# Last layer's edges: one scan per half in place of 14 steps, and one float32 product in place of three bf16 ones

## The reference

```python
msgs = z[edge_dst] @ Wd + z[edge_src] @ Ws + edge_weight[:, None] * ww[None, :] + bm
agg = jax.ops.segment_max(msgs, edge_dst, num_segments=n)
```

## Time and profile before

| | |
|---|---|
| median of three runs | 5489.27 us (5487.87 to 5501.67) |
| the profiled execution | 5497.03 us |
| its span, first to last instruction | 5495.1 us |
| granted TensorE clock, mean over the span | 0.679 |
| the stage of the change | from 4320.9 us to 5420.9 us |

### The profile page before, as it was taken

How to read it: one execution, slowest core, us unless ns; L and a number is a source line. 1 busy time by engine, 2 the same in 40 slices (tenths; PEclk the granted TensorE clock), 3 DMA queues, 4 the chain that set the end, 5 groups by cost and what they waited for, 6 DMA issues and landing times. The chain is left out here.

```text
span 5495.1 us, 57053 instructions
## 1 busy us (share of the span) xinstructions
PE 1987.8 (36%) x9749; PEld 986.7 (18%) x9749; DVE 3681.4 (67%) x8459; ACT 1834.0 (33%) x5828; POOL 3746.1 (68%) x2991
## 2 busy tenths in 40 slices
PE   2699999997600000000020000000002445566555
PEld 1354444443300000000010000000001212222222
DVE  9676666664578878878875666666666545555555
ACT  0333333332338878877820000000001312222221
POOL 0688888887177777777536888888883365556563
PEclk9899999999855555555555555555555777777777
DMA  9555555555337666665635555555552223222222
GB/s 403 154 105 98 102 92 101 101 92 107 95 101 261 226 239 220 241 246 217 233 130 166 169 169 175 176 169 169 170 174 89 64 85 95 91 90 92 90 92 72
DMA packets 283515, 819.47 MB, mean 149 GB/s; under 512 B 63270, under 2 KB 178486, under 8 KB 271251
## 3 DMA queue, kind: packets, MB, share of 16 engines
q1 hardware_dynamic: 99250, 504.98, 25.0%
q0 software_dynamic: 171504, 252.10, 21.1%
q10 hardware_dynamic: 12528, 60.37, 2.7%
HBM read 368.73 MB, written 448.51 MB: 149 GB/s over the span
## 5 line engine op out<-in xcount | busy, mean ns | idle before, releaser
L1864 POOL DMA_INDIRECT arena<-table,arena x784 | 989.9, 1263 | 238.8 <-issue 238.8
L624 POOL DMA_INDIRECT tab<-arena x560 | 988.5, 1765 | 188.8 <-issue 142.7
L746 PE MATMUL psum<-arena 128*128 128x512 bf16 (+1 forms) x4704 | 957.9, 359 | 0.0
L2348 POOL DMA_INDIRECT arena<-table,arena x676 | 651.3, 963 | 425.7 <-issue 201.8
L1514 PE MATMUL psum<-ident,arena 128*128 128x128 f32 x15 | 3.7, 425 | 2525.1 <-DVEq L1542 2525.1
L1287 POOL DMA_INDIRECT arena<-table,arena x588 | 713.1, 1213 | 189.5 <-issue 177.4
L2411 PE MATMUL psum<-arena 128*128 128x512 bf16 x2025 | 588.5, 443 | 378.4 <-issue 272.6
L1333 ACT ACTIVATE arena<-arena 128x128 f32<-128x128 f32 x1974 | 598.5, 388 | 187.4 <-DVE arena L1441 141.9
L1441 DVE SCALAR_TENSOR_TENSOR arena<-arena 128x512 f32<-128x512 f32 x728 | 545.1, 749 | 13.8 <-issue 1.5
L746 PEld LDWEIGHTS psum<-arena 128*128 128x128 bf16 x4704 | 435.8, 99 | 479.8 <-issue 35.6
L1514 PEld LDWEIGHTS psum<-ident,arena 128*128 128x128 f32 x15 | 2.7, 212 | 2525.7 <-DVEq L1542 2525.5
(11 more groups left out here) (406 smaller groups left out, 4207.0 us busy)
## 6 DMA issues: line engine op xcount, KB each, us to landing
rows<-arena SPq DMA_DIRECT2D x56, 3808.0 KB
arena<-seg_rows SPq DMA_DIRECT2D x112, 896.0 KB
rows<-arena SPq DMA_DIRECT2D x56, 1008.0 KB
seg_rows<-arena ACTq DMA_DIRECT2D x28, 1792.0 KB
rows<-arena SPq DMA_DIRECT2D x56, 896.0 KB
arena<-table,arena POOLq DMA_INDIRECT x2048
arena<-src_lanes SPq DMA_DIRECT2D x56, 448.0 KB
tab<-arena POOLq DMA_INDIRECT x560
```

Source lines behind the costliest of these rows:

```text
L624: eng.indirect_dma_start(out=m.tabs[j], out_offset=bass.IndirectOffsetOnAxis(ap=idx[g][:, k:k + 1], axis=0), in_=rows[g][:, k, 0:D], in_of ...
L746: t = eng.matmul(ps[:, c, 0:w], part[n // 2 % PAIRS][:, n % 2, :], hot[n % HOTS][:, lo:lo + w], start=False, stop=False, skip_group_check= ...
L1864: eng.indirect_dma_start(out=kv[k][:, j, :], out_offset=None, in_=m.table2, in_offset=bass.IndirectOffsetOnAxis(ap=idx[k][:, j:j + 1], axi ...
L2348: eng.indirect_dma_start(out=feat[h][:, j, :], out_offset=None, in_=m.table3, in_offset=bass.IndirectOffsetOnAxis(ap=idx[h][:, j:j + 1], a ...
```

## The change

The messages of a half lie feature by feature, with 15 places each: place 0 carries the last maximum of the other half, places 1 to 14 are the edges. One `tensor_tensor_scan` over all 128 x 15 places of a partition (add the reset, take the maximum with the message) gives all states of the half; a reset of -1e30 at place 0 separates the features. ScalarE spreads the resets over the features (`spread_resets`) and writes the states back edge by edge for the store (`turn_back`). The one-hots become float32, and each block's product is one float32 matmul with the table itself; `split` and its three tiles go. ScalarE's order in a turn becomes: scalings of half 0, states of the last half, resets, eviction, indices of half 0, scalings of half 1, states of half 0, resets, indices of half 1 (`next_indices` is `stage` renamed). In VectorE's `half` one one-hot stands ahead of the scan and the others behind it.

```diff
--- before.py
+++ after.py
...
-        msg = A(HALF, D)
+        msg = A(D, HALF + 1)
+        maxima = [A(D, HALF + 1) for _ in range(2)]
         rows = [A(HALF, D) for _ in range(2)]
         tab = A(NB, D)
-        parts = [A(NB, D, dt=BF16) for _ in range(3)]
         keys = A(BATCH, dt=F16)
-        hot = [A(BATCH, dt=BF16) for _ in range(NB)]
+        hot = [A(BATCH) for _ in range(NB)]
         turned_rows = A(BATCH)
-        resets, vals, act_vals = A(BODY), A(BODY), A(BODY)
+        resets = [A(D, HALF + 1) for _ in range(2)]
+        act_vals = A(BODY)
...
                 def store(i, h):
-                    hold(eng, scanned, i * BODY + (h + 1) * HALF + 1)
+                    hold(eng, turned_back[h], i + 1)
                     eng.dma_start(lanes(m.rows3)[:, bass.ds(i * BODY + h * HALF, HALF), :], rows[h]).then_inc(stored[h], 16)
 
+                for h in range(2):
+                    eng.nop().then_inc(stored[h], 16)
...
-                def split():
-                    for k, (a, b) in enumerate(TAB_HALF):
-                        eng.wait_ge(tab_in[k], 16)
-                        eng.activation(parts[0][:, a:b, :], tab[:, a:b, :], ACT.Copy).then_inc(high_made, 1)
-                    for k, (a, b) in enumerate(TAB_HALF):
-                        eng.wait_ge(rest_made, k + 1)
-                        eng.activation(parts[1][:, a:b, :], tab[:, a:b, :], ACT.Copy).then_inc(mid_made, 1)
-
-                def stage(i, h, before):
+                def next_indices(i, h, before):
...
+                        if not isinstance(i, int):
+                            eng.wait_ge(found_summed, i * FOUND - FOUND + 1)
...
+                def spread_resets(i, h):
+
+                    hold(eng, scanned, 2 * i + h)
+                    eng.activation(resets[h][:, :, 1:HALF + 1],
+                                   spread(m.reset[:, bass.ds(i * BODY + h * HALF, HALF)], 1, [P, D, HALF]), ACT.Copy).then_inc(spread_out[h], 1)
+
+                def turn_back(i, h):
+
+                    eng.wait_ge(scanned, 2 * i + h + 2)
+                    eng.wait_ge(stored[h], 16 * i + 16)
+                    eng.activation(rows[h], maxima[h][:, :, 1:HALF + 1].rearrange("p f t -> p t f"), ACT.Copy).then_inc(turned_back[h], 1)
+
+                eng.wait_ge(begun, 2)
+                spread_resets(0, 0)
+                spread_resets(0, 1)
                 scale(0, 0, HALF)
-                split()
-                stage(0, 0, HALF)
+                next_indices(0, 0, HALF)
                 scale(0, 1, HALF)
-                stage(0, 1, HALF)
+                turn_back(0, 0)
+                spread_resets(1, 0)
+                next_indices(0, 1, HALF)
                 with eng.Fori(1, TURNS) as i:
                     scale(i, 0, HALF)
-                    stage(i, 0, i * HALF + HALF)
-                    scale(i, 1, HALF - FOUND)
+                    turn_back(i - 1, 1)
+                    spread_resets(i, 1)
                     eng.wait_ge(hot_used, i * NB + NB)
                     eng.wait_ge(turned, i)
                     eng.activation(turned_rows, found, ACT.Copy).then_inc(evicted, 1)
-                    stage(i, 1, i * (HALF - FOUND) + HALF)
+                    next_indices(i, 0, i * HALF + HALF)
+                    scale(i, 1, HALF - FOUND)
+                    turn_back(i, 0)
+                    spread_resets(i + 1, 0)
+                    next_indices(i, 1, i * (HALF - FOUND) + HALF)
+                turn_back(TURNS - 1, 1)
...
-                eng.wait_ge(low_made, 2)
+                for k in range(2):
+                    eng.wait_ge(tab_in[k], 16)
...
-                        for p, part in enumerate(parts):
-                            t = eng.matmul(found, part[:, b, :], hot[b], start=(b == 0 and p == 0), stop=(b == NB - 1 and p == 2))
-                        t.then_inc(hot_used, 1)
...
                 f = Steps(eng, begun)
-                f.then(eng.memset(rows[1][:, HALF - 1, :], -BIG))
-                eng.engine_nop().then_inc(weighed, 1)
+                for h in range(2):
+                    f.put(eng.memset(resets[h], -BIG))
+                f.then(eng.memset(maxima[1], -BIG))
+                eng.engine_nop().then_inc(found_summed, 1)
...
-                def split():
-
-                    for k, (a, b) in enumerate(TAB_HALF):
-                        eng.wait_ge(high_made, k + 1)
-                        eng.tensor_tensor(tab[:, a:b, :], tab[:, a:b, :], parts[0][:, a:b, :], ALU.subtract).then_inc(rest_made, 1)
-                    for k, (a, b) in enumerate(TAB_HALF):
-                        eng.wait_ge(mid_made, k + 1)
-                        eng.tensor_tensor(parts[2][:, a:b, :], tab[:, a:b, :], parts[1][:, a:b, :], ALU.subtract).then_inc(low_made, 1)
...
-                def stage(i):
-                    eng.wait_ge(scanned, i * BODY + 1)
-                    eng.nop(nofuse=True)
-                    eng.tensor_copy(resets, m.reset[:, bass.ds(i * BODY, BODY)]).then_inc(marked, 1)
-                    eng.tensor_copy(vals, m.val[:, bass.ds(i * BODY, BODY)]).then_inc(marked, 1)
-                    eng.wait_ge(marked, 2 * i + 2)
-
                 def half(i, h, n, before, hots):
 
+                    eng.wait_ge(scanned, 2 * i + h + 1)
+                    eng.tensor_copy(msg[:, :, 0], maxima[1 - h][:, :, HALF]).then_inc(carried, 1)
                     eng.wait_ge(landed[h], 16 * before)
                     eng.wait_ge(scaled, 2 * i + h + 1)
-                    eng.wait_ge(scanned, i * BODY + h * HALF + 1)
-                    eng.tensor_tensor(msg[:, 0:n, :], feat[h][:, 0:n, :], scaled_w[:, 0:n, :], ALU.add).then_inc(summed, 1)
+                    by_edge = msg.rearrange("p f t -> p t f")
+                    eng.tensor_tensor(by_edge[:, 1:n + 1, :], feat[h][:, 0:n, :], scaled_w[:, 0:n, :], ALU.add).then_inc(summed, 1)
                     if n < HALF:
                         eng.wait_ge(turned, i + 1)
-                    for j in range(n, HALF):
-                        s = h * HALF + j
-                        eng.scalar_tensor_tensor(out=msg[:, j, :], in0=m.edge_w[:, :], scalar=vals[:, s:s + 1],
-                                                 in1=rows_found[:, j - n, :], op0=ALU.mult, op1=ALU.add).then_inc(weighed, 1)
+                        eng.wait_ge(vals_staged, i + 1)
+                        for j in range(n, HALF):
+                            s = h * HALF + j
+                            eng.scalar_tensor_tensor(out=by_edge[:, j + 1, :], in0=m.edge_w[:, :], scalar=act_vals[:, s:s + 1],
+                                                     in1=rows_found[:, j - n, :], op0=ALU.mult, op1=ALU.add).then_inc(found_summed, 1)
+                    for hot_of in hots[:1]:
+                        one_hot(*hot_of)
+                    eng.wait_ge(spread_out[h], i + 1)
+                    eng.wait_ge(carried, 2 * i + h + 1)
                     eng.wait_ge(summed, 2 * i + h + 2)
-                    for j in range(HALF):
...
-                        eng.wait_ge(scanned, i * BODY + s + 1)
-                        if j == 0 and not (isinstance(i, int) and i == 0):
-                            eng.wait_ge(stored[h], 16 * i)
-                        if j == n:
-                            eng.wait_ge(weighed, i * FOUND + 1)
-                        eng.scalar_tensor_tensor(out=rows[h][:, j, :], in0=rows[h][:, j - 1, :] if j else rows[1 - h][:, HALF - 1, :],
-                                                 scalar=resets[:, s:s + 1], in1=msg[:, j, :], op0=ALU.add, op1=ALU.max).then_inc(scanned, 1)
-                        if j < len(hots):
-                            one_hot(*hots[j])
+                    if n < HALF:
+                        eng.wait_ge(found_summed, i * FOUND + 1)
+                    eng.wait_ge(turned_back[h], i)
+                    eng.tensor_tensor_scan(maxima[h].rearrange("p f t -> p (f t)"), resets[h].rearrange("p f t -> p (f t)"),
+                                           msg.rearrange("p f t -> p (f t)"), -BIG, ALU.add, ALU.max).then_inc(scanned, 1)
+                    for hot_of in hots[1:]:
+                        one_hot(*hot_of)
 
...
-                stage(0)
...
-                split()
...
-                eng.wait_ge(scanned, TURNS * BODY + 1)
-                f.then(eng.tensor_copy(m.lane_end[:, 0:D], rows[1][:, HALF - 1, :]))
+                eng.wait_ge(scanned, 2 * TURNS + 1)
+                f.then(eng.tensor_copy(m.lane_end[:, 0:D], maxima[1][:, :, HALF]))
```

More of the change, by code:

```diff
@@ L2301, in layer3_edges @@
         tab_in = [sem(f"table_landed{k}") for k in range(2)]
[L2302 removed]
         keys_in, hot_made, hot_used = sem("keys_landed"), sem("one_hots_made"), sem("one_hots_used")
         evicted, turned = sem("rows_evicted"), sem("rows_turned")
[L2305 removed]
         vals_staged, scaled = sem("weights_staged"), sem("weights_scaled")
[L2307 removed]
+        spread_out = [sem(f"resets_spread{h}") for h in range(2)]
```

(8 more changed lines are left out.)

8 lines of the change are left out of this document (1 added, 7 removed).

## The result

| | kernel before | kernel changed |
|---|---|---|
| median of 4 runs | 5488.57 us (5484.47 to 5501.67) | 5534.23 us (5529.28 to 5546.23) |
| profiled execution | 5497.03 us, span 5495.1 | 5546.23 us, span 5544.5 |
| stage, first gather to last | 4321.9 to 5397.1: 1075.2 us | 4331.0 to 5456.3: 1125.3 us |
| turn, mean of 26 | 39.17 us | 1048.30 / 26 = 40.32 us |

The ratio is 1.0082, 95% interval 1.0059 to 1.0106: slower by 0.8%. The 50.1 us between the first gather and the last are the whole difference of the spans, 49.4 us.

What follows compares the result with a forecast made beforehand. It took GpSimd's gathers plus 8.3 us of waits per turn as the stage's bound. A turn of 30.9 + 3.7 = 34.6 us saves 119 us, the ends 8: 5489 - 127 = 5362, rounded 5360 us; range 5265 to 5580.

Steps and rivals of the forecast that it cites:

- GpSimd's own turn: GpSimd's time per turn without its waits, 24 gathers of 1.25 us included: 30.9 us, before and after the change.
- E: Rival, slower: gathers wait while float32 one-hots are written, 6.5 us per turn; +42 us, 5530 us; chance 0.03.
- fall of 4.6 us per turn: The stage's turn goes from 39.17 to 34.6 us; 26 turns give 119 us less.
- tail: GpSimd's wait per turn for late signals, eviction, staging and first gather: 3.7 us in place of 8.3.
- The late signals: VectorE's signalling operations per turn fall from 61 to 33; priced per signalling instruction, its idle time falls by 26/61.
- A: Rival, faster: GpSimd never waits and the 8.3 us per turn go altogether; -224 us, 5265 us; chance 0.17.
- Scan 4.3 us: VectorE: each of two scans per turn over 128x1920 takes 4.3 us, 8.6 us for both.
- One-hot 0.47: VectorE: a one-hot of 512 elements written in float32 takes 0.47 us; 25 add 2.0 us per turn.
- D: Rival, slower: float32 one-hots take 0.68 us on VectorE, turn 44 us; +117 us, 5605 us; chance 0.07.
- C: Rival, slower: TensorE becomes the bound, turn 45.3 us at 1.2 GHz throughout; +151 us, 5640 us; chance 0.21.
- B: Rival: the stall belongs to gathers in flight, not VectorE's instruction count; only the ends gain, 5480 us; chance 0.14.
- The ends: Start and end of the stage: -7.5 us by dropping the three-way split, nothing from the last turn; 8 us less.

Runs made afterwards that it cites:

- Scans alone: Changed kernel with the bf16 one-hots, three-way split and three bf16 products of before: 5449.0 us (kernel before beside it 5249.2) and 5444.5 us (5500.7).
- messages in PSUM: Changed kernel with the scan reading its messages from PSUM and its resets from SBUF, float32 one-hots and products kept: 5302.0 us (ratio 1.0097), again 5331.1 us (1.0026).
- PSUM and bf16: Changed kernel with the scan's messages in PSUM, bf16 one-hots and three bf16 products per block: 5254.0 us (ratio 0.9997), 5242.3 us (0.9972), 5517.2 us (1.0030).
- unstruck: Kernel before, unchanged, in the faster of its two conditions: 5253.7 us profiled, 30.30 us per turn; struck means the condition where it takes about 5490 us.
- The scan in 8 pieces: Changed kernel with each scan made as eight over 16 features: 5443.1 us (ratio 0.9912); with bf16 one-hots and three bf16 products, 5294.3 us (1.0072).

## Why the prediction failed

**Its direction was wrong; its range, 5265 to 5580 us, held the 5534.** The step that failed is GpSimd's own turn, which the sum, the forecast and every rival but E carried over as 30.9 us (24 gathers x 1.25 = 30.0, and 0.9 more). It became 24 x 1.675 = 40.2 us. Scans alone and the messages in PSUM show that the scan's second SBUF input makes 7.3 us of it and the float32 one-hots 2 to 3. The forecast's fall of 4.6 us per turn became a rise of 1.15.

**Why I missed it.** I costed the scan by VectorE's time alone, and looked for a claim on GpSimd only in the one-hots. The steps that the scan replaces had two SBUF inputs too, but at 0.35 us each they held a gather for little in that trace (three of 676 took over 3 us); one instruction of 4.15 us holds it for all of that. I then gave rival E 0.03 since gathers took 963 ns beside today's one-hots: a row of bf16 one-hots can't show what float32 ones do. E's 5530 us was right to 4 us by luck: it had 6.5 us per turn of one-hots and a tail of 3.7 us, where there are 2.7 of one-hots, 7.6 of scans and no tail.

**The late signals.** I read 8.3 us of waits per turn as the kernel's and forecast 3.7 us to stay. In the changed kernel 4.3 / 26 = 0.2 us stayed, but my reason, fewer of VectorE's signals, is refuted by PSUM and bf16, which loses as much with 35 of them as the kernel before with 61. A's claim, a turn at GpSimd's floor and 5265 us, is what PSUM and bf16 and the kernel before show unstruck, not the changed one. The change took away one loss of 8.9 us per turn and put another of some 10 in its place, which is the measured +1.15 us per turn, 29.9 of the 50 us. The other 20 lie behind the window: the last gather ends 14.6 us after it in the changed kernel and ended 5.2 us ahead of its end in the kernel before. Against an unstruck kernel before, 5534 to 5249 would be 5% slower; that pair was never run side by side.

**The terms that held.** Scan 4.3 us, measured 4.15. One-hot 0.47, measured 0.487, which ends D, and is near the estimate from the Trainium skill (VectorE: DVE Perf Modes, The perf-mode tier table), 0.43. TensorE's share was 730.75 / 26 = 28.1 us per turn at a granted 0.80, so C did not come. B neither, in its form: GpSimd's waits went. (75 x 0.21 to 0.42 is 15.8 to 31.5 us, not 16.0 to 32.0; no term used it.)

**The terms that were off and cost nothing here.** The sum into the layout by features took 3.23 and 2.34 us, not 2.02 and 1.49; I had not priced its output's stride. The copies that turn the maxima back took 3.31 us, not 1.7 (the spreads did, 1.69). ScalarE's turn was 18.0 us, not 15.5. VectorE and ScalarE have 15 and 22 us of idle time in the turn, so neither counts. The ends were to give 8 us: behind the last gather it was 98.0 us and is 88.2, and the start of the stage moved by 9.1 between the two traces, which the stages ahead of it explain as well (it lies between 4309.6 and 4332.6 over all runs).

**A version that beats both.** None does in both conditions. Messages in PSUM with bf16 products is level with the kernel before in one unstruck set and 0.3% faster in the other, 0.3% slower where it is struck. Scans alone is 1.0% faster struck and 3.8% slower unstruck. The scan in 8 pieces is 0.9% faster struck, and with bf16 0.7% slower unstruck; neither was run in the other condition.

**What stays open.** What makes single instructions of VectorE, TensorE and SyncE late. All kernels whose time the condition raises have gathers near 0.95 us; those whose gathers are held have fewer such stretches, or hide them. That the number of TensorE's products decides (theory 4) was not tested in a struck set. The traces of struck runs also lack most of the semaphore changes that DMAs make: between 4400 and 5150 us, 1,303 are recorded in the first profile of before and 10,704 in the one at 5253.7. This marks the whole set and not the kernel: the changed kernel has 3,596 to 4,248 in its three traces and scans alone 2,166 when struck, while no trace of an unstruck set has under 8,646. Names of waits suffer with it: the idle time before the eviction in scans alone is put down to the products when unstruck (223.3 us) and to a DMA for which it doesn't wait when struck (326.8). So what a struck trace names is weak evidence, and how much time passes between two instructions is the better one. The Trainium skill (NOTIFIC — the notification-queue block, Overflow: three behaviours, one of which stalls the engine) says that the block that writes trace records holds its producers back rather than lose a record inside it. By that the profiler itself could make the lateness, though it would not explain that records are missing; no run here separates it.

## What to carry to other kernels

Before merging small VectorE instructions into one long one, list its inputs. Here two in SBUF held the gather that GpSimd was issuing until the scan ended, and float32 one-hots of one input held some as well, so price such an instruction on GpSimd's account too; with one scan input in PSUM no gather was held by the scan. Ask of every idle time that a profile shows without a releaser whether the same kernel shows it in another run, before a change is credited with its removal. When a floor of one engine's issue rate carries the sum, look at what runs beside it after the change, not at its mean before.

## What was not expected of the hardware

- A gather of 0.944 us took 4.6 to 5.0 us beside a scan of 4.15 us with both inputs in SBUF, and 0.94 beside the same scan with one input in PSUM.
- The holding can outlast one instruction: 6.54 us beside 19 short ones in a row, each 0.35 to 0.48 us long; or hardly happen (1.01 to 1.03 us), in another half of the same turn.
- A float32 sum over 1,792 elements took 2.02 us with its output in order and 3.22 with its output strided by 15 elements into SBUF; the same stride in PSUM took 2.03.
- ScalarE's copy of 1,792 float32 took 1.69 us writing a broadcast input in order of features, and 3.31 us reading across features.
